# Two attention-and-feed-forward layers in one program: the bias table computed in the inner layer, stack loads counted by head pair, loads and stores moved between queues, and the expert tail's selected rows laid out tile by tile

## The reference

```python
xn = layernorm(x)
x = x + latent_attention(xn) + ternary_ffn(xn)      # layer 0
xn = layernorm(x)
x = x + biased_attention(xn) + experts(xn)          # layer 1

# latent_attention: 16 heads of 16, k and v from a latent of 64, causal softmax, W_O
# ternary_ffn: h = silu(x w1 s1) * (x w2 s2); h = gelu(h h1 s); h = gelu(h h2 s); h w3 s   (256 -> 1024 -> 1024 -> 1024 -> 256)
# biased_attention: logits = q k * scale + pos_bias[h, |i - j|], 16 heads, softmax, Wout.
#   pos_bias comes from a table: 4 filters of 101 taps over a ramp of 128, mixed by Wpos
# experts: rows in groups of 16; for each of 64 experts (16 x 4) the row of the group with the largest
#   controller logit is selected, sent through relu(row f1 + bias) f2 (inner size 64), and added back at its place
```

## Time and profile before

| | us |
|---|---|
| median of 3 runs | 1992.14 |
| lowest, highest | 1989.74, 1992.73 |
| the profiled execution, its own time | 1986.88 |
| its span, first to last instruction | 1984.8 |
| mean granted clock | 0.954 |
| PE busy | 1733.1 (87%) |
| DVE busy | 1151.9 (58%) |
| ACT busy | 1064.0 (54%) |
| POOL busy | 978.1 (49%) |

### The profile page before, as it was taken

The page is one execution under the profiler, slowest core; times in us unless marked ns, Lnnn a source line. Parts: engine busy times, 40 slices in busy tenths (PEclk is TensorE's granted clock), DMA queues, the critical chain, the costliest instruction groups (busy, mean ns, idle before and its releaser), DMA issues. The chain is left out here.

```text
span 1984.8 us, 32309 instructions
## 1 busy us (share of the span) xinstructions
PE 1733.1 (87%) x11015; PEld 1135.6 (57%) x11015; DVE 1151.9 (58%) x2519; ACT 1064.0 (54%) x1471; POOL 978.1 (49%) x736
## 2 busy tenths in 40 slices
PE   4989888887999999999996967788888788868999
PEld 3455554544788888888885753333334334336566
DVE  5665666662243433534434428988888898826345
ACT  1555555555632323323222325988889899965542
POOL 1444444432434434434342434887887787855102
PEclk7999999998999999999998987999999999978999
DMA  3333333323521201201101172323223232108356
GB/s 115 97 107 90 89 95 94 95 75 122 172 91 40 69 24 58 79 27 58 52 33 51 42 256 76 86 75 90 92 65 107 66 82 80 33 13 314 108 160 207
DMA packets 119261, 182.85 MB, mean 92 GB/s; under 512 B 14197, under 2 KB 73077, under 8 KB 119162
## 3 DMA queue, kind: packets, MB, share of 16 engines
q1 hardware_dynamic: 114300, 175.31, 29.0%
q10 hardware_dynamic: 4224, 4.19, 0.6%
q0 software_dynamic: 640, 2.10, 0.3%
HBM read 90.72 MB, written 39.91 MB: 66 GB/s over the span
## 5 line engine op out<-in xcount | busy, mean ns | idle before, releaser
L839 POOL TENSOR_TENSOR l_prob<-l_prob,l_bias 128x1024 f32<-128x1024 f32 x192 | 452.9, 2379 | 100.9 <-ACT l_prob L998 100.1
L1278 POOL TENSOR_TENSOR f_hl<-f_full,f_hh 128x512 fp32r<-128x512 f32 x192 | 248.1, 1292 | 411.4 <-DVE f_hh L1316 271.0
L1054 DVE CUSTOM_DVE_ANT_0 l_slot<-l_slot,l_bias 128x512 f32<-128x512 f32 x512 | 339.6, 713 | 23.4 <-PE l_slot L1138 23.3
L1001 ACT ACTIVATE l_prob<-l_prob 128x1024 f32<-128x1024 f32 x256 | 273.7, 1076 | 0.5 <-POOL l_prob L839 0.5
L493 DVE TENSOR_REDUCE l_peak<-l_slot 128x2 f32<-128x256 f32 (+3 forms) x256 | 206.2, 821 | 107.1 <-PE l_slot L585 104.7
L1366 PE MATMUL f_ps<-f_hh,f_hi_h 128*128 128x512 f32 x1024 | 260.3, 390 | 3.6 <-ACT f_hh L1290 2.6
L1366 PE MATMUL f_ps<-f_hl,f_hi_h 128*128 128x512 f32 x1024 | 258.3, 389 | 0.0
L397 ACT ACTIVATE l_prob<-l_slot 128x1024 f32<-128x1024 f32 (+3 forms) x256 | 175.3, 706 | 96.9 <-PE l_slot L604 93.8
L1366 PEld LDWEIGHTS f_ps<-f_hh,f_hi_h 128*128 128x128 f32 x1024 | 192.0, 188 | 47.0 <-issue 3.3
L1366 PEld LDWEIGHTS f_ps<-f_hl,f_hi_h 128*128 128x128 f32 x1024 | 192.2, 188 | 39.8
L1298 ACT ACTIVATE f_full<-f_ps,f_h_s 128x512 f32<-128x512 f32 x128 | 86.8, 684 | 235.3 <-PE f_ps L1366 217.0
(11 more groups left out here) (228 smaller groups left out, 2817.0 us busy)
## 6 DMA issues: line engine op xcount, KB each, us to landing
l_stacks<-l_parts SPq DMA_DIRECT2D x384, 128.0 KB, 2.6
f_raw<-in_L_ffn_h_w SPq DMA_DIRECT2D x16, 512.0 KB, 4.2
f_raw<-in_L_ffn_h_w SPq DMA_DIRECT2D x32, 256.0 KB, 2.6
e_w<-in_L_ffn_f SPq DMA_DIRECT2D x32, 256.0 KB, 2.9
l_bias<-ext SPq DMA_DIRECT2D x16, 448.0 KB, 8.0
l_x_in<-in_L_attn_x SPq DMA_DIRECT2D x8, 512.0 KB, 3.9
xh<-l_xh SPq DMA_DIRECT2D x8, 512.0 KB, 2.6
xl<-l_xl SPq DMA_DIRECT2D x8, 512.0 KB, 2.6
```

Source lines behind the costliest of these rows:

```text
L839: return eng.tensor_tensor(probs(n), src, bias[:, h:h + 2, j * P:j * P + T], ALU.add)
L1001: act.activation(probs(n), probs(n), ACT.Exp).then_inc(p_exp.sem, 1)
L1054: ins = dve.tensor_tensor_reduce(src, src, bias[:, 4 * g + 2 * pr + a, t * P:t * P + T], 1.0, 3 * NEG, ALU.add, ALU.max, peak[:, g, a, pr, ...
L1278: pool.tensor_tensor(t.hl[layer % 2][:, o], t.full[:, n % 2], t.hh[layer % 2][:, o].bitcast(F32), ALU.subtract).then_inc(self.h_lo.sem, 1)
```

## The change

It does these things:

- The counter of the stack loads is split in two, one for each head pair; `score` waits for 3 loads at n % 4 == 0. In batch 0, for quads 0 and 1, SP issues the loads of pair 0 and ACT those of pair 1 (`shared`).
- Layer 0: the x rows of batch 1 are issued by SP right after the stores of batch 0's `xh` and `xl`, ahead of the stacks. In the last batch ACT copies the turned mix straight to the high part, and DVE makes the low part from PSUM; POOL and the extra copy have no share.
- The bias table's products move from steps 3 and 5 of the gate/up layer to steps 2 and 4 of the first inner layer, the wait for its copies to the second inner layer; `ext` moves from `attn` to `tanh`; SP loads `attn` first, and issues the pieces before it waits for the table.
- Opening of layer 1: POOL's second memset of `stacks` and DVE's four low weight parts move into the new block (q and k at its start, v and o after the low part of batch 0's x).
- The last store of the biased attention is issued by ACT.
- `sel` is written tile by tile: for each tile of 128 rows 64 experts x 2 x 4 groups, side by side as `choose` makes them (512 values in a row). An expert's 256 columns are then 32 runs of 8 values, and the stationary operand of a transpose has a stride of 4 values (16 bytes).

```diff
-        stack_in = [sem(f"stack_in{g}", 6, unit=16) for g in range(QUADS)]
+        stack_in = [[sem(f"stack_in{g}{pr}", 3, unit=16) for pr in range(2)] for g in range(QUADS)]
...
+        def shared(b, n):
+            return opening(b) and n < 2
+        def load_stack(eng, n, pr):
+            src = parts[64 * (n % 2) + 32 * pr:64 * (n % 2) + 32 * pr + 32, n // 2].bitcast(F32)
+            for s, (first, step) in enumerate(((1, 1), (0, 2), (1, 2))):
+                eng.dma_start(stacks[s:P:4, :, 2 * n + pr].bitcast(F32),
+                              src[:, first:first + step + 1:step]).then_inc(stack_in[n][pr].sem, 16)
...
+                        if opening(b):
+                            load_rows(sp, 1)
...
+                    if kind == "stack" and shared(b, n):
+                        wait(act, low_ready, n // 2 + 1, b)
+                        if n == 0:
+                            act.wait_ge(keyed.sem, 16)
+                        load_stack(act, n, 1)
...
+                    if kind == "mix_copy" and closing(b):
+                        act.copy(mixt[:, 0], slot("mix_turn", 0)[:]).then_inc(mh_ready.sem, 1)
+                    if kind == "mix_high" and closing(b):
+                        wait(dve, mh_ready, 1, b)
+                        dve.tensor_tensor(mixt[:, 1], slot("mix_turn", 0)[:], mixt[:, 0].bitcast(F32), ALU.subtract)\
+                           .then_inc(ml_ready.sem, 1)
...
-                        if n % 8 == 0:
-                            wait(pe, stack_in[g], 6, b)
+                        if n % 4 == 0:
+                            wait(pe, stack_in[g][pr], 3, b)
...
-        pool.memset(stacks[:, 1].bitcast(F32), 0.0).then_inc(blank.sem, 1)      # last batch of the feed-forward
+            pool.memset(stacks[:, 1].bitcast(F32), 0.0).then_inc(blank.sem, 1)  # new block, after minus
...
+                if kind == "store" and b == B - 1:
+                    wait(act, out_ready, TT // 2, b)
+                    act.dma_start(out_d[b].rearrange("(t p) d -> p t d", p=P), out_sb[:]).then_inc(out_saved.sem, 16)
...
+                    if n == KD - 1 and opening(b):
+                        low_weights(dve, 2)
...
+            low_weights(dve, 0)
             turns(dve, emit)
...
             load_x(B - 1)
+            load_attn(B - 1)
             sp.wait_ge(f.out_saved.sem, f.out_saved.at(1, B - 2))
             table.load_fir(sp)
+            pieces(B - 1)
             table.store(sp)
             sp.wait_ge(table.saved, 16)
-            load_attn(B - 1)
-            pieces(B - 1)
...
-                if n == 4:
+                if n == KH + 3:
                     table.first_copy(act)
-                if n == KH - 2:
+                if n == KH + 6:
                     table.copies(act)
...
-            opening.weights(dve)
...
-                if o == 3:
+                if o == KH + 2:
                     table.first_product(pe)
-                if o == 5:
+                if o == KH + 4:
                     table.products(pe)
-                if o == KH - 1:
+                if o == 2 * KH:
                     pe.wait_ge(table.ext_ready, 2)
...
-            halves = sel[:, n % 2].rearrange("p e (a g) -> p e a g", a=2)
-            return halves[:, :, :, bass.ds(b * (TT * G // 2) + n // 2 * (G // 2), G // 2)]
+            tiles = sel[:, n % 2].rearrange("p e g -> p (e g)").rearrange("p (r a g) -> p r a g", a=2, g=G // 2)
+            return tiles[:, bass.ds((b * TT + n // 2) * E, E)]
...
+def spread(sel):
+    return sel[:].rearrange("p k e g -> p k (e g)").rearrange("p k (r e g) -> p k r e g", e=E, g=P // NE)
+def tile_of(pair):
+    step = P // NE // 2
+    first = pair // step * E * 2 * step + pair % step
+    return slice(first, first + (E * 2 - 1) * step + 1, step)
...
-            return sel[:, :, 2 * v + a, :]
+            return spread(sel)[:, :, :, 2 * v + a]
...
-                                ins = pe.transpose(turn_banks[half][u % 2][:, at:at + P], flat[k][:, g // 2::GROUPS // 2], ident[:])
+                                ins = pe.transpose(turn_banks[half][u % 2][:, at:at + P], flat[k][:, tile_of(g // 2)], ident[:])
```

More of the change, by code:

```diff
@@ L268, in _, with load_rows @@
             def _(sp):
+                def load_rows(sp, b):
+                    wait(sp, xn_ready, TT, b - 1)
+                    sp.dma_start(x_in[:], x_d[b].rearrange("(t p) d -> p t d", p=P)).then_inc(x_loaded.sem, 16)
                 def emit(kind, b, n, i):
[L270 to L272 removed]
+                    if kind == "x_load" and not opening(b) and not opening(b - 1):
+                        load_rows(sp, b)
                     if kind == "x_low":
@@ L282, in emit @@
                             sp.wait_ge(keyed.sem, 16)
-                        for pr in range(2):
-                            src = parts[64 * (n % 2) + 32 * pr:64 * (n % 2) + 32 * pr + 32, n // 2].bitcast(F32)
-                            for s, (first, step) in enumerate(((1, 1), (0, 2), (1, 2))):
-                                sp.dma_start(stacks[s:P:4, :, 2 * n + pr].bitcast(F32),
-                                             src[:, first:first + step + 1:step]).then_inc(stack_in[n].sem, 16)
+                        for pr in range(1 if shared(b, n) else 2):
+                            load_stack(sp, n, pr)
                     if kind == "maxima":
@@ L327, in emit @@
                                            ALU.subtract).then_inc(low_ready.sem, 1)
-                    if kind == "mix_low":
+                    if kind == "mix_low" and not closing(b):
                         wait(pool, mh_ready, 1, b)
@@ L918, in emit @@
                         sp.wait_ge(keyed.sem, 16)
-                    for pr in range(2):
-                        src = parts[64 * (n % 2) + 32 * pr:64 * (n % 2) + 32 * pr + 32, n // 2].bitcast(F32)
-                        for s, (first, step) in enumerate(((1, 1), (0, 2), (1, 2))):
-                            sp.dma_start(stacks[s:P:4, :, 2 * n + pr].bitcast(F32),
-                                         src[:, first:first + step + 1:step]).then_inc(stack_in[n].sem, 16)
-                if kind == "store":
+                    for pr in range(1 if shared(b, n) else 2):
+                        load_stack(sp, n, pr)
+                if kind == "store" and b != B - 1:
                     wait(sp, out_ready, TT // 2, b)
@@ L943, in _ @@
             for g in range(QUADS):
-                sp.wait_ge(stack_in[g].sem, stack_in[g].at(6, B - 1))
+                for pr in range(2):
+                    sp.wait_ge(stack_in[g][pr].sem, stack_in[g][pr].at(3, B - 1))
             next_opening.sp(sp)
@@ L983, in emit @@
                         for g in (n, n + 1):
-                            wait(act, stack_in[g], 6, b - 1)
+                            for pr in range(2):
+                                wait(act, stack_in[g][pr], 3, b - 1)
                     act.copy(parts[:, n // 2, 1 + n % 2], bank(kind, n, b)).then_inc(high_ready.sem, 1)
@@ L1001, in emit @@
                     act.activation(probs(n), probs(n), ACT.Exp).then_inc(p_exp.sem, 1)
+                if kind == "stack" and shared(b, n):
+                    wait(act, low_ready, n // 2 * 2 + 2, b)
+                    if n == 0:
+                        act.wait_ge(keyed.sem, 16)
+                    load_stack(act, n, 1)
                 if kind == "heads_copy":
```

33 lines of the change are left out of this document (18 added, 15 removed).

## The result

The changed kernel takes 1963.57 us (median of 4 runs, 1956.55 to 1965.49), the kernel before 1991.0 (4 runs): a ratio of 0.9854, with an interval of 0.9835 to 0.9874. The forecast was 1963.3. That it is so near is partly luck: three terms of the sum were off, and their errors cancel. The profiled execution took 1956.55 us, the shortest of the four, with a span of 1954.7.

A forecast was written before the change was run, and what follows sets the result against it. Stages follow one another and engines meet between, so savings count where they shorten a stage's closing or opening chain. Terms 16.6 + 4.7 + 1.2 + 0.3 + 6.0 = 28.8 us, from median 1992.1 to 1963.3; range 1947 to 1971.

The forecast's parts named there:

- The feed-forward's table: Last feed-forward batch: moving the bias table's products hides PE's wait for their load; 16.6 us gained, bounds 12.4 and 18.4.
- the stall: First inner layer of the last feed-forward batch: PE waits 1.2 us, plus 0.6 for a late `c_fir`; 1.8 taken.
- a late piece 0 makes ACT's row of outputs 3 us late: Inner layer: piece 0 lands 10 to 11 us in, delaying ACT's outputs some 3 us; PE stalls 1.2 us.
- Opening of layer 0: Layer 0's start: fewer SP issues before the first score and no DVE wait for x; 4.7 us, bounds 2.0 and 5.5.
- ACT comes to its loads only after rounding W_O: Layer 0's opening: rounding ends at 25.64, so pair 1 is issued by 27.6, covered by four scores of pair 0.
- End of layer 0: End of layer 0's attention: PE starts 2.0 us earlier, then ACT is late; 1.2 us gained, bounds 0.5 and 1.25.
- Opening of layer 1: Layer 1's start: PE starts earlier but bias loads later, so the first score gains 0.3 us; bounds -1 and 4.6.
- SP's store issue at 1168.77 is last, and PE starts at about 1169.7: Layer 1's opening: without POOL's memset and DVE's low parts, SP's store is last and PE starts 2.6 us earlier.
- Last store: End of layer 1's attention: with the store on ACT, PE starts `choose` 6.0 us earlier; bounds 4.0 and 6.5.
- Layout: Tail: transposes' weight loads and products over runs of eight keep their time; 0 us gained.
- each value still is alone in its 16 bytes, so the strided row is nearest: Transposes in `apply`: eight weight loads keep the strided 1.25 us rather than the contiguous 0.85; 0 gained.
- The rival with the contiguous rate: Transposes in `apply` load at the contiguous rate, 12.8 us more gained, total 1950.5; chance 0.25.

The follow-up runs named there:

- the first profile: Profiled execution of the changed kernel in its first comparison with the kernel before: 1956.55 us.
- the first comparison: The changed kernel beside the kernel before, four runs each: 1963.57 us against 1991.0, ratio 0.9854.
- the second: The changed kernel, unedited, measured again against the kernel before: 1964.54 us, ratio 0.9873.

## Why the prediction was right, point by point

**The feed-forward's table: 16.6 forecast, 18.2 measured**, inside the bounds. The load lands in time, the added work is 2.9 us for the 2.7 worked out, and the mis-sized term is the stall: 1.8 were taken and none came. The step behind it, that a late piece 0 makes ACT's row of outputs 3 us late and so PE wait, failed. Piece 0 came 10 us into the layer as reckoned, but ACT, which has time between outputs, rounded it and still had the small product copied 1.6 us before PE came.

**Opening of layer 0: 4.7 forecast, 2.8 measured.** The wait for x went, as said. The 2.0 for three issues fewer did not come, and the step that failed is "ACT comes to its loads only after rounding W_O". ACT's loads do stand behind the rounding in its code, but their issue doesn't wait for it: the first goes out with SP's at 23.13, the roundings are at 23.60 and 23.92. Behind it is a second error: the sum gave pair 1's copies no price, and beside them pair 0's third load lands 4.7 us behind its issue rather than 2.6. The run without the share shows it, and there the 2.0 us come.

**End of layer 0: 1.2 forecast.** From ACT's copy of the turned mix to the feed-forward's first product it takes 10.4 to 11.1 us with the edit (eleven profiles), and 12.15, 11.31 and 11.44 without: 0.9 on the mean. The mechanism was right: the low part takes 1.23 us on DVE, and ACT's last copy follows its rounding without a gap, so ACT is what is late next.

**Opening of layer 1: 0.3 gained by the forecast, 3.3 lost on the mean of the runs** (1.7 to 5.4), beyond the bound of -1. The step that failed is "SP's store issue at 1168.77 is last, and PE starts at about 1169.7". PE's sequencer came to the meeting point 1.6 us behind SP, held by its branch. So PE starts 1.1 us earlier and not 2.6, and the bias loads are 2.4 us later and not 0.9; in the other profiles with this opening PE starts 0.3 to 0.7 us earlier, and the bias loads come 2.8 to 3.2 later. The rest of the chain, that the backlog behind the bias loads sets the first score, was right: the 15 us from bias issue to score held in the first profile (14.6 to 18.1 in the others), and moving the bias loads moved the score. How much of the loss reaches the end of the stage stays open: from SP's store to the last copy the new openings took 615.7 to 622.7 us, the old ones 615.8 to 623.1.

**Last store: 6.0 forecast, 6.3 measured**, in every kernel that has the edit.

**Layout: 0 forecast, 5.6 us measured on the mean** (66.1 to 60.5). The step that failed is the choice between the bounds: "each value still is alone in its 16 bytes, so the strided row is nearest". 16 bytes cost 209 ns, between the two rows. The rival with the contiguous rate had the better direction, but its 12.8 us were not to be had either: with loads of 141 ns the turns take 61.7 us, and the trace puts that down to DVE, which waits 10.8 us for POOL's sum and so for late loads of x and the attention. The Trainium skill ("SBUF — State Buffer", section "Specifications (TRN2)") has a penalty for each crossing into a new line of 16 bytes and full speed from two accesses in a line. The runs don't bear this out for weight loads: two values in a line cost the same 209 ns as one, and 512 bytes cost more than 16 although both cross with every value.

**The sum.** Against the terms, the two openings gave 5.5 us less than forecast (2.8 - 3.3 for 4.7 + 0.3), the layout 5.6 more and the table 1.6 more. The median came out right by that, and the direction by the table and the last store, which are 24.5 of the 27 us. The terms as measured add up to 30.5 us, though, and the medians differ by 27.4 in the first comparison and by 24.7 in the second. Where the other 3 to 6 us went is open; the long stretches, which differ by more than that between executions, can hold them.

## What to carry to other kernels

Issuing loads from a second queue isn't free because its engine is: compare the GB/s with one queue and with two, and if they hardly differ, the second queue only lets later data fly beside the data that the next step waits for. An engine's DMA issue need not wait for the work ahead of it in that engine's order. Where a late engine is moved out of a meeting point, look up when each other engine's sequencer arrives there, PE's too, before counting the gain. Data that the first step needs go first in the queue, then those of the next step in time, and bulk loads that are needed much later go last of all: with the bias loads behind the stacks the wait moved to the x rows behind them.

## What the runs showed of the hardware

- Weight loads of 128 x 128 f32 by stride: 4 bytes 141 ns, 8 bytes 209, 16 bytes 209, 512 bytes 256.
- A moving operand of 256 columns in runs of 8 values takes 379 ns, as side by side; in runs of 2, one every 512 bytes, 455.
- ACT's write of 128 x 512 values whose successive values go 512 bytes apart takes 1.2 us rather than 0.64.
- Copies inside the memory on chip moved 192 to 200 GB/s from one queue (DMA share 0.76 to 0.77) and 193 to 215 from two (0.90 to 0.96). A load of 128 KB landed 2.6 us after its issue with one queue and 4.1 with two, at the median.
- An issue of ACT's queue went out at 23.13, ahead of two roundings of 23.60 and 23.92 that stand before it in the code.
- PE's sequencer came to the end of the block 3.6 us behind its last product (1146.0 to 1149.6), 3.6 to 4.5 in the fourteen profiles. What ends just ahead of it is a branch of 4.9 to 5.9 us, which took the other engines 0.04 to 0.06.
